# Categories in natural order, and the first batch's x tile found by a smallest key, in a per-category matrix product on one core

## The reference

```
# x (128, 128, 512) f32; itok (128,) int32 in 0..30; W (32, 512, 512); b (32, 512)
selected_W = W[cat_ids]
selected_b = b[cat_ids]
y = jnp.einsum('bti,bio->bto', x, selected_W) + selected_b[:, None, :]
return x + y
```

## Time and profile before

| | |
|---|---|
| median of 3 runs | 365.95 us (365.12 to 366.31) |
| the profiled execution, its span | 367.44 us, 365.6 us |
| TensorE busy | 355.9 us, 97% of the span, 1554 instructions |
| GpSimd busy | 268.6 us, 73% |
| VectorE, ScalarE busy | 172.1 us, 148.9 us |
| DMA | 109.53 MB, 300 GB/s on average |
| chain that ended last | TensorE 82%, GpSimd 8%, DMA 5% |

### The profile page before, as it was taken

How to read it: one execution, slowest core, us unless ns; L and a number is a source line. 1 busy time by engine, 2 the same in 40 slices (tenths; PEclk the granted TensorE clock), 3 DMA queues, 4 the chain that set the end, 5 groups by cost and what they waited for, 6 DMA issues and landing times.

```text
span 365.6 us, 7498 instructions
## 1 busy us (share of the span) xinstructions
PE 355.9 (97%) x1554; PEld 292.2 (80%) x1554; DVE 172.1 (47%) x277; ACT 148.9 (41%) x264; POOL 268.6 (73%) x146
## 2 busy tenths in 40 slices
PE   5999998999999999999999999999999999999996
PEld 3778886888888888888888888888888888888884
DVE  4563464445445444454454454444544545544542
ACT  4662354333444344343343443443343425434420
POOL 3587888899988888885578674679878886788000
PEclk9999999999999999999999999999999999999999
DMA  5799999899989999999787988779999899786632
GB/s 207 271 341 377 399 322 317 280 343 366 323 304 326 353 294 342 337 350 321 278 303 286 349 298 304 239 264 316 382 313 301 296 372 353 261 300 196 196 115 86
DMA packets 43112, 109.53 MB, mean 300 GB/s; under 512 B 4801, under 2 KB 5058, under 8 KB 38210
## 3 DMA queue, kind: packets, MB, share of 16 engines
q1 hardware_dynamic: 37152, 68.89, 52.5%
q0 software_dynamic: 5632, 39.85, 32.2%
q10 hardware_dynamic: 290, 0.33, 0.3%
HBM read 75.50 MB, written 33.55 MB: 298 GB/s over the span
## 4 chain that ended last, share of the span: by engine, by line
PE 82%; POOL 8%; DMA 5%; issue 3%; SPq 0%; ACT 0%; POOLq 0%; DVEq 0%; DVE 0%
PE pA L451 82%; POOL wl L269 4%; DMA bb<-bias 3%; POOL wh L265 2%; DMA wr<-w 1%; POOL wl L251 1%; POOL wr L239 1%; SPq L129 0%; ACT wh L309 0%; POOL wr L226 0%; POOL bb L143 0%; POOL wr L216 0%; DVEq L36 0%; POOLq L138 0%; POOLq L137 0%
## 5 line engine op out<-in xcount | busy, mean ns | idle before, releaser
L388 DVE TENSOR_TENSOR os<-pA,bb 128x512 f32<-128x512 f32 x129 | 88.6, 687 | 175.5 <-PE pA L451 173.3
L291 ACT ACTIVATE xh<-xs 128x512 fp32r<-128x512 f32 x128 | 81.0, 633 | 195.3 <-PE pA L451 116.1
L269 POOL TENSOR_TENSOR wl<-wr,wh 128x2048 fp32r<-128x2048 f32 x30 | 138.7, 4624 | 2.5
L451 PE MATMUL pA<-wh,xl 128*128 x508 | 136.0, 389 | 1.7 <-POOL wl L269 1.4
L451 PE MATMUL pA<-wl,xh 128*128 x508 | 135.8, 389 | 0.0
L451 PE MATMUL pA<-wh,xh 128*128 x508 | 135.8, 389 | 0.0
L451 PEld LDWEIGHTS pA<-wh,xl 128*128 128x128 f32 x508 | 95.2, 188 | 22.1 <-issue 2.5
L451 PEld LDWEIGHTS pA<-wh,xh 128*128 128x128 f32 x508 | 95.3, 188 | 19.9
L451 PEld LDWEIGHTS pA<-wl,xh 128*128 128x128 f32 x508 | 95.3, 188 | 19.8
L348 DVE TENSOR_TENSOR xl<-pT,xh 128x512 fp32r<-128x512 f32 x128 | 87.2, 681 | 10.2 <-ACT pT L294 10.1
L265 POOL TENSOR_SCALAR wh<-wr 128x2048 fp32r<-128x2048 f32 x30 | 57.5, 1917 | 30.4 <-PE pA L451 28.3
(11 more groups left out here) (45 smaller groups left out, 21.9 us busy)
## 6 DMA issues: line engine op xcount, KB each, us to landing
xs<-xt SPq DMA_DIRECT2D x127, 256.0 KB, 5.3
out<-os SPq DMA_DIRECT2D x127, 256.0 KB, 5.0
wr<-w POOLq DMA_DIRECT2D x30, 1024.0 KB, 7.5
bb<-bias POOLq DMA_DIRECT2D x7, 1024.0 KB, 9.9
wr<-w SPq DMA_DIRECT2D x2, 512.0 KB, 5.1
wr<-w SPq DMA_DIRECT2D x1, 1024.0 KB, 7.6
bb<-bias POOLq DMA_DIRECT2D x2, 256.0 KB, 6.1
bb<-bias POOLq DMA_DIRECT2D x1, 512.0 KB, 11.7
```

The source lines that it names most:

```text
L269: eng.tensor_tensor(wl[:, at], wr[:, c % NR, :], wh[:, at].bitcast(f32), ALU.subtract).then_inc(s_wp if c == 2 else s_w, 1)
L291: eng.activation(xh[:, i % NH, :, :], xs[:, i % NX, :, :], ACT.Copy).then_inc(s_xh, 1)
L388: eng.tensor_tensor(os[:, i % NO, d0:d1], pA[i % NA][:, d0:d1], bb[:, bass.ds(at + d0, d1 - d0)], ALU.add).then_inc(s_fin, 1)
L451: mm = eng.matmul(pA[i % NA][:, :], xp[:, i % NH, k, :], wp[:, bass.ds(at + k * D, D)], start=(n == 0), stop=(n == 3 * KT - 1))
```

## The change

The rotation is taken out. Categories are processed from 0 to 31, so weights and bias are at fixed addresses and no register is needed for them. Which batch is first is no longer known beforehand: VectorE makes a key 128 x category + batch for every batch (L300 of the changed kernel), takes the smallest and masks it to the batch number `t0`, ahead of the rest of the sort. SyncE loads it to a register and issues x tile 0. The first weights are issued by ScalarE as its first instructions, and `idr` by SyncE.

Work moves too. GpSimd adds the eye of all four chunks of category 0, and makes wh of category 1, which ScalarE did. xl of tile 0 is made from `xs` instead of `pT`. The weights of category 1 are issued behind x tile 3 instead of x tile 2. The bias of categories 1 to 3 is one load, and category 1 is released only when it has landed. The product of `below` stands ahead of batch 0, and four warm products (L395) instead of one follow the sort. TensorE starts batch 0 only when all tables are there. The loop over i covers batch 0.

```diff
-            cat = category(eng, "sc")
-            c = cat(0)
-            for n in range(2):
-                eng.dma_start(raw(0, 2 * n, 2 * n + 2),
-                              W[bass.ds(c, 1), :, 2 * n * D:(2 * n + 2) * D].rearrange("a p d -> (a p) d"))\
-                   .then_inc(s_w0[n], 16)
-            c = cat(1)
+            eng.dma_start(idr[:, :], ids.rearrange("(a n) -> a n", a=1)).then_inc(s_id, 16)
+            first = eng.alloc_register("first")
+            eng.wait_ge(s_t0, 1)
+            eng.load(first, t0[0:1, 0:1])
+            x_load(eng, 0, bass.ds(eng.snap(first, min_val=0, max_val=B - 1), 1))
...
-                if i >= NX:
-                    eng.wait_ge(s_pt, i - NX + 1)
+                if i == NX:
+                    eng.wait_ge(s_xl, 1)
+                elif i > NX:
+                    eng.wait_ge(s_pt, i - NX)
...
-                if i == 2:
-                    eng.dma_start(wr[:, 1, :], W[bass.ds(c, 1), :, :].rearrange("a p d -> (a p) d")).then_inc(s_w1, 16)
+                if i == 3:
+                    eng.dma_start(wr[:, 1, :], W[1, :, :]).then_inc(s_w1, 16)
...
             def load(c):
-                eng.dma_start(wr[:, c % NR, :], W[bass.ds(cat(c), 1), :, :].rearrange("a p d -> (a p) d"))\
-                   .then_inc(s_wr[c % NR], 16)
+                eng.dma_start(wr[:, c % NR, :], W[c, :, :]).then_inc(s_wr[c % NR], 16)
                 if c % NB == 0:
-                    bias_load(eng, c0, c, c + NB, s_bb[c // NB])
+                    bias_load(eng, c, c + NB, s_bb[c // NB])
...
-            for k in range(2):
+            for k in range(KT):
                 eye = diagonal(0, k, k + 1)
-                eng.wait_ge(s_w0[0], 16)
+                eng.wait_ge(s_w0[k // 2], 16)
...
+                    bias_load(eng, 1, NB, s_bb[0])
...
+                eng.wait_ge(s_ri, KT + c)
+                eng.tensor_scalar(wh[:, at], wr[:, c % NR, :], 1.0, 1.0, ALU.mult, ALU.mult).then_inc(s_wh, 1)
+                eng.wait_ge(s_wh, c)
+                if c > 1 and c % NB == 0:
+                    eng.wait_ge(s_bb[c // NB], 16)
+                eng.tensor_tensor(wl[:, at], wr[:, c % NR, :], wh[:, at].bitcast(f32),
+                                  ALU.subtract).then_inc(s_wp if c == 1 else s_w, 1)
                 if c == 1:
-                    for h in range(2):
-                        at = chunk(c, 2 * h, 2 * h + 2)
-                        eng.wait_ge(s_rh, KT + 2 * c - 1 + h)
-                        eng.tensor_tensor(wl[:, at], raw(c, 2 * h, 2 * h + 2), wh[:, at].bitcast(f32),
-                                          ALU.subtract).then_inc(s_wp, 1)
-                    eng.wait_ge(s_wp, 3)
+                    eng.wait_ge(s_wp, 2)
                     load(3)
-                    bias_load(eng, c0, 2, NB, s_bb[0])
-                    eng.wait_ge(s_b0[1], 16)
+                    eng.wait_ge(s_bb[0], 16)
                     eng.sem_inc(s_w, 1)
...
+                elif c + NR < C:
+                    eng.wait_ge(s_w, c + 1)
+                    load(c + NR)
...
-            eng.dma_start(idr[:, :], ids.rearrange("(a n) -> a n", a=1)).then_inc(s_id, 16)
-            x_load(eng, 0, slice(0, 1))
+            for n in range(2):
+                eng.dma_start(raw(0, 2 * n, 2 * n + 2), W[0, :, 2 * n * D:(2 * n + 2) * D]).then_inc(s_w0[n], 16)
...
+                if i == 0:
+                    return
...
-            high(0)
...
-                if k < 2:
-                    eng.wait_ge(s_ri, k + 1)
-                else:
-                    eng.wait_ge(s_rd, k - 1)
+                eng.wait_ge(s_ri, k + 1)
...
+                if k == 0:
+                    high(0)
             for i in range(1, B):
                 high(i)
-                if i == 2:
-                    c = 1
-                    eng.wait_ge(s_ri, 2 + c)
-                    for h in range(2):
-                        eng.activation(wh[:, chunk(c, 2 * h, 2 * h + 2)], raw(c, 2 * h, 2 * h + 2), ACT.Copy)\
-                           .then_inc(s_rh, 1)
...
-            link(eng.tensor_tensor(rot[:, 0, :], idr[:, :], idr[0:1, 0:1].to_broadcast([1, 128]), ALU.subtract))
-            link(eng.tensor_single_scalar(rot[:, 1, :], rot[:, 0, :], C - 1, ALU.bitwise_and))
-            eng.tensor_copy(rotb[:, :], rot[:, 1, :]).then_inc(s_row, 1)
+            link(eng.tensor_single_scalar(idm[:, :], idr[:, :], C - 1, ALU.bitwise_and))
+            eng.tensor_copy(idb[:, :], idm[:, :]).then_inc(s_row, 1)
+            eng.wait_ge(s_io, 1)
+            link(eng.scalar_tensor_tensor(out=key[:, :], in0=idm[:, :], scalar=float(B), in1=iot[0:1, :],
+                                          op0=ALU.mult, op1=ALU.add))
+            link(eng.tensor_reduce(low1[:, :], key[:, :], AX.X, ALU.min))
+            eng.tensor_single_scalar(t0[:, :], low1[:, :], B - 1, ALU.bitwise_and).then_inc(s_t0, 1)
...
             def low(i):
                 eng.wait_ge(s_xh, i + 1)
-                eng.wait_ge(s_pt, i + 1)
-                eng.tensor_tensor(xl[:, i % NH, :, :], pT[i % NT][:, :, :], xh[:, i % NH, :, :].bitcast(f32),
+                if i == 0:
+                    x = xs[:, 0, :, :]
+                else:
+                    eng.wait_ge(s_pt, i)
+                    x = pT[i % NT][:, :, :]
+                eng.tensor_tensor(xl[:, i % NH, :, :], x, xh[:, i % NH, :, :].bitcast(f32),
...
+            eng.wait_ge(s_tab, 2)
+            eng.tensor_scalar(tv[:, :], tc[:, :], 1.0, float(D), ALU.subtract, ALU.mult).then_inc(s_tab, 1)
+            eng.wait_ge(s_bat, 3)
+            eng.tensor_scalar(tn[:, :], pS[0:1, 0:C], 1.0, None, ALU.add).then_inc(s_tab, 1)
             low(0)
...
-            eng.wait_ge(s_cst, 2)
-            eye_w(2)
-            eye_w(3)
...
-            warm(1)
+            eng.wait_ge(s_hot, 3)
+            eng.matmul(pS[0:1, 0:C], ones[:, 0:1], below[:, :], start=True, stop=True).then_inc(s_bat, 1)
+            warm(4)
...
-            eng.wait_ge(s_xh, 1)
-            for n, (p, k) in enumerate(first):
-                if n == 4:
-                    eng.wait_ge(s_tab, 2)
-                    row(0)
...
+            eng.wait_ge(s_tab, 4)
+            for i in range(B):
...
-        "bias": np.concatenate([np.asarray(L0_cond_b)] * 2),
+        "bias": np.ascontiguousarray(L0_cond_b),
```

More of the change, by code:

```diff
@@ L58, in cond_resid @@
         idr = sb("idr", [1, 128], i32)
-        rot = sb("rot", [1, 2, 128], i32)
-        rotb = sb("rotb", [1, 128], bf16)
+        idm = sb("idm", [1, 128], i32)
+        idb = sb("idb", [1, 128], bf16)
+        key = sb("key", [1, 128], i32)
+        low1 = sb("low1", [1, 1], i32)
+        t0 = sb("t0", [1, 1], i32)
         colf = sb("colf", [128, 1], f32)
@@ L92, in cond_resid @@
         s_wr = [sem(f"s_wr{i}") for i in range(NR)]
-        s_b0 = [sem(f"s_b0{i}") for i in range(2)]
+        s_b0 = sem("s_b0")
         s_bb = [sem(f"s_bb{i}") for i in range(C // NB)]
@@ L124, in diagonal, with bias_load @@
             return bass.AP(t.tensor, t.offset, [list(t.ap[0]), [D + 128, k1 - k0], [1, 128]])
-        def category(eng, name):
-            first = eng.alloc_register(f"{name}0")
-            eng.load(first, ids.rearrange("(a n) -> a n", a=1)[0:1, 0:1])
-            eng.reg_alu(first, first, C - 1, ALU.bitwise_and)
-            turn = eng.alloc_register(f"{name}1")
-            def get(j):
-                if j == 0:
-                    return eng.snap(first, min_val=0, max_val=C - 1)
-                eng.reg_alu(turn, first, j, ALU.add)
-                eng.reg_alu(turn, turn, C - 1, ALU.bitwise_and)
-                return eng.snap(turn, min_val=0, max_val=C - 1)
-            return get
-        def bias_load(eng, c0, j0, j1, done):
+        def bias_load(eng, j0, j1, done):
             at = slice(j0 * D, j1 * D)
             eng.dma_start(bb[:, at].rearrange("p (c d) -> p c d", c=j1 - j0),
-                          bias[bass.ds(c0 + j0, j1 - j0), :].rearrange("(a c) d -> a c d", a=1)
-                          .to_broadcast([128, j1 - j0, D])).then_inc(done, 16)
+                          bias[j0:j1, :].rearrange("(a c) d -> a c d", a=1).to_broadcast([128, j1 - j0, D]))\
+               .then_inc(done, 16)
         def table(eng, name, src, n, lo, hi, ahead=4):
@@ L341, in _ @@
             eng.tensor_copy(colb[:, :], colf[:, :]).then_inc(s_hot, 1)
+            eng.tensor_scalar(below[:, :], thr[:, :], colf[:, 0:1], None, ALU.is_gt).then_inc(s_hot, 1)
             eng.wait_ge(s_bat, 1)
@@ L417, in _ @@
             at_reg = eng.alloc_register("at")
-            eng.wait_ge(s_xh, 1)
-            for n, (p, k) in enumerate(first):
-                if n == 4:
-                    eng.wait_ge(s_tab, 2)
-                    row(0)
-                if n == 8:
-                    eng.wait_ge(s_hot, 3)
-                    eng.matmul(pS[0:1, 0:C], ones[:, 0:1], below[:, :], start=True, stop=True).then_inc(s_bat, 1)
-                if p == HH:
-                    eng.wait_ge(s_rh, k + 1)
```

(22 more changed lines are left out.)

53 lines of the change are left out of this document (12 added, 41 removed).

## The result

The changed kernel takes 364.04 us (median of 8 runs, 363.04 to 364.62) against 366.13 us for the kernel before (8 runs, 364.68 to 366.84): a ratio of 0.9942, 95% interval 0.9923 to 0.9962, or 2.1 us less. The forecast was 362.9 us, 3.06 us less, in a range of 361.7 to 365.2 us. The profiled execution took 364.17 us with a span of 362.3 us; the forecast of the span was 362.5 us. So the end of the profiled execution was forecast to 0.2 us, the median was missed by 1.1 us, and the forecast gain was half again too large. Why all three can be true is the main thing that the experiments had to settle.

The account below looks back on a forecast made before the run. An unbroken run of products from 62.54 us set the end, so only TensorE time lost earlier counted. Gains of 1.0, 0.49 and 1.57 us made 3.06 us: 365.95 - 3.06 = 362.9 us, range 361.7 to 365.2 us.

Parts of the forecast that it names:

- no stall, a small margin: Before batch 6: category 1 ready at 26.0 us, wanted at 26.8 us, margin 0.7 us, so TensorE does not wait.
- rival 1: Before batch 6: bias of categories 1 to 3 a little late, costing up to 2.3 us, 363.2 to 365.2 us; 25%.
- rival 2: Before batch 6: that bias much late, at 31.1 us, a 4.4 us stall, net 1.3 us slower, 367.3 us; 7%.
- rival 4: At the start: x tile 0 lands near 9.5 us, batch 0 starts 2 us later than forecast, 364.9 us; 3%.
- rival 3: In batch 0: fast product pitch comes sooner, batch 1 at 12.0 us, category 1 then 0.5 us late, 362.2 us; 20%.
- the conversion of the sum to the median: From profiled execution to median: the whole 3.06 us gain was taken off the median, 365.95 us, giving 362.9 us.
- term 2: At batch 3: TensorE's wait for a late xl of tile 3 goes, gaining 0.49 us.
- term 3: Before batch 18: TensorE's wait for GpSimd's wl of the sixth category goes, gaining 1.57 us.
- A cost counted at nothing: GpSimd's register arithmetic before weight loads: dropping it shortens its 0.80 us gap, counted as no gain since GpSimd has slack.
- term 1: At the start: batch 1's products begin at 13.2 us instead of 14.20 us, gaining 1.0 us.
- The collision of xl and GpSimd: In batch 0: xl of tile 0 shares SBUF ports with GpSimd's wl, ends about 9.75 us, at a price of 0.3 us.

Follow-up runs that it names:

- the second and third trace: The kernel before, unchanged, profiled twice more: 366.11 us (10 runs) and 366.33 us, spans 364.4 and 364.5 us.
- the second trace: Said of the changed kernel: that kernel run again without an edit; 364.06 us (5 runs), ratio 0.9953, span 362.2 us.
- the run with the early xl: Changed kernel with six warm products instead of four, and xl of tile 3 made ahead of batch 0's output: 363.38 us, ratio 0.9922.

## Why the prediction was right, and where its sum was too large

**What held.** The unbroken run of products sets the end, and its beginning moved from 62.54 us to batch 0. The span (362.5 us forecast, 362.3 us measured), the start of batch 1 (13.2 and 13.08 us), the bias landing (25.9 and 25.5 us) and "no stall, a small margin" came as forecast. Rivals 1, 2 and 4 did not happen; rival 3 did not either, but six warm products made it happen, with the counter-move that it named (category 1 then late by 0.3 to 0.6 us) and a larger one that it had missed, xl of tile 3.

**The step that failed: the conversion of the sum to the median.** "I take off the same difference from both" took the whole 3.06 us from 365.95 us. Terms 2 and 3, 0.49 and 1.57 us, were sizes of one execution. In the other two traces of before term 3 was 1.1 and 0.6 us, and term 2 nothing and 0.75 us. The three terms together are the distance from TensorE's new start to GpSimd's arrival, and that arrival was 1.1 to 1.3 us later in the execution read than in the others. From the second and third trace the distance is 2.0 and 2.2 us, the 2.1 us that were measured. Taken off the profiled execution's own time the sum gives 367.44 - 3.06 = 364.4 us, and 364.17 us was measured. The text had noted that the profiled execution lay 1.5 us above the median, but not asked what the 1.5 us were: 1.1 to 1.3 us of them were GpSimd's late arrival, and so stood in these terms. That the median still fell in the range is owed to the range's upper end, which was there for a late bias.

**A row misread.** "GpSimd had stood still for a bias load from 23.27 to 35.0 us" is wrong. The chain books the time from issue to landing; the earlier trace rows show GpSimd at work on wh and wl from 25.22 to 31.85 us. It stood for the end of the load alone, 1.40 us in this trace:

```profile
35.18 1.29 POOL L239 TENSOR_TENSOR wr<-wr,ident 128x512 f32<-128x512 f32 x1 [1.40 <-DMA bb<-bias]
```

In the other two traces it was 1.06 and 0.45 us. Taking that wait out gave 0.2 us.

**A cost counted at nothing.** The registers on GpSimd were 0.50 us for three of the loads and 0.87 us for a fourth, 2.4 us by the sixth category, more than the bias wait. In natural order they do not matter, as the prediction said, and no product waits for GpSimd. In the rotated version of the changed kernel the sixth category was in time by 0.1 to 0.2 us, less than these 2.4 us; no run took them alone out of or into that kernel.

**The start, term 1.** The forecast start of batch 1 came out by luck, from two errors that cancel. x tile 0 was early: the key did not delay the sort as forecast (colf at 3.29 us, not 3.75). The prediction gave every VectorE step 0.32 us, but `key`, which needs no result of `idb`, started 0.14 us behind it (2.46 and 2.60 us). And x landed at 6.91 us, not 7.5. The first product came at 7.76 us instead of 8.2 us, and the third at 8.81 instead of 9.75 us. But the fast pitch came at 13.1 us or later, not at 12.3 us: the ten products from the third on all ran at 0.427 us. Against the other two traces of before, where batch 1 starts at 13.87 and 13.81 us, term 1 is 0.7 to 0.8 us.

**The collision of xl and GpSimd** was real: xl of tile 0 took 0.97 us, in the second trace 1.35 us, against 0.69 us, with GpSimd's wl beside it. In all nine traces of the changed kernel and its variants it took 0.96 to 1.41 us and ended 0.54 or 0.55 us behind GpSimd's wl, whenever it had begun (the prediction had 0.42 us). By the Trainium skill, "SBUF — State Buffer", section "SBUF: two separate sides", the later one waits until the earlier has ended. The traces agree: the end of xl kept the same distance to GpSimd's end, and 0.54 us of the 0.69 us that xl takes alone lay behind it. It cost nothing in the first trace, where the second product ran until then, and 0.2 us in the second.

## What to carry to other kernels

Before a loss is put in a sum, ask which of two arrivals it separates: a wait for the later arrival is worth at most the distance to the earlier one, and losses on the side that arrives first are worth nothing until the other side gets faster. Take the sum off the profiled execution's own time, and when that lies above the median by as much as one of the terms, take a second trace first. A chain piece from a DMA's issue to its landing is not the time that somebody stood still; the idle time in the waiting engine's row is.

## What the runs showed of the hardware

- TensorE's pitch: with an idle time of 0.5 to 1.9 us between the last warm product and batch 0, the pitch turned from 0.43 to 0.23 us between 11.7 and 13.3 us in six traces of the changed kernel and its variants, with one warm product as with four. With that idle time closed it turned between 7.9 and 9.5 us in three of three. The line of granted clock reads full over all of this.
- In nine traces of the changed kernel and its variants the bias load of 256 KB that follows 1 MB of weights took 6.7 to 8.6 us from issue to landing, the one of 768 KB (seven traces) 7.9 to 9.3 us, one of 1792 KB 11.2 us: seven times the bytes took 2.6 to 4.5 us more.
- The time that lies outside the span was 1.74 to 1.84 us in 53 runs of before, 1.87 to 2.90 us in the changed kernel's 8, and 1.98 to 3.09 us in the run with the early xl, which is why spans gained more there than times. GpSimd at fixed addresses alone raised it to 1.89 to 1.98 us. What fills it no profile shows, and it stays open.
